# Block 1's square root on ScalarE, block 0 normalised by VectorE and GpSimd side by side, and an order planned with narrower margins

## The chip, the cores and the metric

One core of one Trainium2 chip runs the kernel. The metric is the device time of one execution in microseconds, as the median of several runs. Five engines work in parallel and are tied together by semaphores: TensorE (PE, matmuls; its weight loads are listed apart as PEld), VectorE (DVE), ScalarE (ACT), GpSimd (POOL) and SyncE (SP), which issues most of the DMAs.

## What is computed

```
xn  = layernorm(x)                                   # x: 2 x 4096 x 256, eps 1e-5
h   = tanh(xn @ W1.T + b1);  s = h @ w2 + b2         # scores
e   = exp(s - max(s));  ctx = cumsum(e * xn) / cumsum(e)
att = tanh(concat(ctx, xn) @ Wc.T + bc)
ffn = (silu(xn @ Wg.T) * (xn @ Wu.T)) @ Wd.T         # int32 weights / 127, 768 hidden
out = x + att + ffn
```

All 8192 tokens lie on one core. Float operands are split into a high and a low half-precision part, so that one product in f32 becomes two or three matmuls in f16.

## The kernel before

The tokens are cut into 16 blocks of 512, a block into two pairs of 128-token tiles. The work of a block is cut into steps, each of one engine, named by a kind, the block and a number:

- B (VectorE) takes mean and variance of a pair of tiles, R (VectorE) starts the reciprocal root and T (GpSimd, three Newton rounds) ends it; Ln (ScalarE) or Lp (GpSimd) normalises a pair.
- Lb (TensorE) transposes a pair of blocks 0 and 1, Xh (ScalarE) and Xl (VectorE) take its high and its low half out of PSUM. From block 2 on the halves are made by Xh and Xm (GpSimd) and turned by DMA (Tx, SyncE).
- Ss (ScalarE) seeds a PSUM bank with the bias b1, S (TensorE, 12 matmuls of 256 columns) adds xn @ W1, Th (ScalarE) takes tanh, Sv (VectorE) the product with w2 into a score.
- Gg and Gu (TensorE, 4 matmuls of 512 columns each, six of either kind in a block) are the gate and up products, Sg (ScalarE) silu, H (VectorE) their product, Hh and Hl (ScalarE, VectorE) its halves, D (TensorE) the down product, Da (VectorE) adds it.
- C, Cs, Ct, Ca, N, Sc, Ch, Cl are the same for the context and the second tanh; W1h, W1l, Wgh, Wuh, Wdh turn weights into half precision, K... check them.

The order of each engine's steps is no loop. A planner (`Plan`) runs when the kernel is built: `due_times` gives every step a due time, `needs` says what it must wait for, `STEP` holds its engine, how long it keeps the engine and when its result is seen. `take_one` gives a free engine the earliest due step that is ready. `SLACK` is a margin that a step must leave after its needs once the plan's time is past `STEADY`; `SENT` and `X_SENT` are the times at which weights and x are taken to be there. The steps are then issued in this order on each engine, in order and with semaphore waits; TensorE's order also decides which of the 8 PSUM banks a product uses, and so which earlier step must have freed it.

Ahead of the plan stands a start written out by hand. TensorE runs `WARM` matmuls on constants, spreads the rows b1 and w2 over the partitions by two products with ones (`to_every`), runs `FILL` more matmuls, and then takes the plan's first steps Lb(0,0), Lb(0,1), S(0,0), S(0,1), Gg(0,0). VectorE takes block 0's statistics (`stats_first`), its root with ScalarE's Sqrt in the middle (`root_first`) and normalises its four tiles (`normalise_first`). ScalarE has Sqrt, Copy and Tanh/Silu to run, and loads a table of functions for Sqrt at its start and one for Silu (step Tb).

## Time and profile before

| | us |
|---|---|
| median of 3 runs | 393.72 |
| lowest, highest | 392.94, 393.87 |
| the profiled execution, its own time | 393.06 |
| its span in the profile | 391.1 |
| TensorE busy in the span | 385.9 |

The profile lists one execution. Its own time, 393.06 us, holds 1.96 us that lie around the span of the program's instructions, and stands 0.66 us below the median of the runs. TensorE is busy in 99% of the span; the end of a matmul in the profile is modelled, so the start of the next instruction is the firmer number.

### The profile page before, as it was taken

To read this page: it belongs to the slowest core of one execution; us is meant where nothing else is said; L and a number is where in the kernel's file an instruction comes from. 1 tells how busy PE (TensorE), PEld (TensorE's weight loads), DVE (VectorE), ACT (ScalarE), POOL (GpSimd) and SP (SyncE) were. 2 spreads that over 40 slices of the span, in tenths; PEclk is the share of its full clock that TensorE was granted. 3 is DMA by queue.
4 is the path that set the end of the run, shared out by engine and by line. 5 is a ranking of instruction groups with operands and counts; after the bars stand their busy time and mean duration, and the time that the engine had idled before them with its cause. 6 is when DMAs were issued, how large, how long until landed. Compare 5 with 4: busy or idle time off the path is not lost.

```text
span 391.1 us, 7885 instructions
## 1 busy us (share of the span) xinstructions
PE 385.9 (99%) x2740; PEld 268.7 (69%) x2740; DVE 297.5 (76%) x632; ACT 235.6 (60%) x434; POOL 210.1 (54%) x289
## 2 busy tenths in 40 slices
PE   8999999999999999999999999999999999999996
PEld 4556676757566686866877676767677676676765
DVE  6799998999996997876769966777676765754351
ACT  4766576689985659786556575364553644536250
POOL 1487586874629989794335405866456554502000
PEclk9999999999999999999999999999999999999999
DMA  8944525576834232475210005043231220100001
GB/s 275 348 158 69 137 53 134 106 189 89 201 72 96 54 83 81 116 165 97 76 34 29 27 28 164 28 128 87 58 72 55 90 85 26 54 28 28 28 28 61
DMA packets 54945, 36.56 MB, mean 93 GB/s; under 512 B 31858, under 2 KB 50292, under 8 KB 54900
## 3 DMA queue, kind: packets, MB, share of 16 engines
q1 hardware_dynamic: 54608, 35.73, 35.5%
q8 instruction: 24, 0.39, 0.4%
...
q14 instruction: 21, 0.17, 0.1%
HBM read 20.19 MB, written 8.45 MB: 73 GB/s over the span
## 4 chain that ended last, share of the span: by engine, by line
PE 97%; DVE 2%; issue 0%; DVEq 0%
PE bank L707 44%; PE bank L743 41%; PE bank L763 9%; PE bank L1381 1%; DVE ex L1121 0%; DVE stats L951 0%; PE bank L700 0%; PE bank L1377 0%; DVE veps L980 0%; DVE xt L1091 0%; DVE bank L1116 0%; DVE sg L1413 0%; PE bank L813 0%; DVE mv L955 0%; PE bank L819 0%
## 5 line engine op out<-in xcount | busy, mean ns | idle before, releaser
L743 PE MATMUL bank<-xt,narrow 128*128 128x512 f16 x768 | 177.3, 379 | 0.0
L743 PEld LDWEIGHTS bank<-xt,narrow 128*128 128x128 f16 x768 | 75.2, 98 | 75.4 <-DVE wide L1121 0.2
L707 PE MATMUL bank<-narrow,wide 128*128 128x256 f16 x792 | 96.4, 273 | 0.0
L707 PE MATMUL bank<-narrow,xt 128*128 128x256 f16 x768 | 92.8, 273 | 0.3 <-DVE xt L1091 0.3
L707 PEld LDWEIGHTS bank<-narrow,xt 128*128 128x128 f16 x768 | 75.0, 98 | 19.0 <-DVE xt L1091 0.6
L1258 POOL TENSOR_TENSOR wide<-ex,wide 128x512 f16<-128x512 f32 x32 | 39.4, 1248 | 87.6 <-ACT wide L909 87.6
L888 ACT ACTIVATE sg<-bank 128x512 f32<-128x512 f32 x96 | 57.2, 596 | 46.3 <-PE bank L743 45.6
L1116 DVE SCALAR_TENSOR_TENSOR bank<-bank,sg 128x512 f32<-128x512 f32 x96 | 66.1, 694 | 24.4 <-PE bank L743 21.3
L707 PEld LDWEIGHTS bank<-narrow,wide 128*128 128x128 f16 x792 | 77.5, 98 | 9.4
L895 ACT ACTIVATE wide<-bank 128x512 f16<-128x512 f32 x90 | 53.3, 596 | 47.7 <-DVE bank L1116 39.3
L1121 DVE TENSOR_TENSOR wide<-bank,wide 128x512 f16<-128x512 f32 x90 | 60.5, 678 | 9.9 <-ACT wide L895 8.6
L1139 DVE TENSOR_TENSOR_SCAN ex<-rows,ex 128x512 f32<-128x512 f32 x32 | 56.5, 1767 | 0.7 <-POOL ex L1230 0.7
L1230 POOL TENSOR_TENSOR ex<-ex,rows 128x512 f32<-128x512 f32 x32 | 44.8, 1401 | 9.2 <-DMA rows<-scratch 6.9
L1225 POOL TENSOR_TENSOR ex<-xt 128x512 f32<-128x512 f16 x32 | 44.6, 1395 | 0.2
L1125 DVE TENSOR_TENSOR xres<-bank,xres 128x512 f32<-128x512 f32 (+1 forms) x33 | 22.0, 667 | 26.4 <-PE bank L707 26.3
L841 ACT ACTIVATE bank<-every 128x512 f32<-128x512 f32 (+1 forms) x65 | 38.3, 594 | 0.0
L763 PE MATMUL bank<-narrow,wide 128*128 128x256 f16 x312 | 38.3, 273 | 0.0
L902 ACT ACTIVATE bank<-bank 128x512 f32<-128x512 f32 (+1 forms) x33 | 18.8, 569 | 31.0 <-PE bank L707 31.0
L763 PEld LDWEIGHTS bank<-narrow,wide 128*128 128x128 f16 x312 | 30.5, 98 | 7.4
L1130 DVE TENSOR_TENSOR xres<-bank,xres 128x512 f32<-128x512 f32 x28 | 19.3, 688 | 18.2 <-ACT bank L902 18.1
L1101 DVE CUSTOM_DVE_ANT_0 bank<-bank,every 128x256 f32<-128x256 f32 x64 | 25.4, 446 | 4.1 <-ACT bank L882 4.1
L1244 POOL TENSOR_TENSOR xt<-xnat,xt 128x512 f16<-128x512 f32 x14 | 16.9, 1226 | 11.3 <-ACT xt L869 11.3
...
## 6 DMA issues: line engine op xcount, KB each, us to landing
...
xt<-xt SPq DMA_TRANSPOSE x56, 2.5
...
wide<-in_wc SPq DMA_DIRECT2D x1, 512.0 KB, 11.1
```

The costliest lines, as they stand in the source:

```text
L707: return pe.matmul(dst, lhs, rhs, start=False, stop=stop, skip_group_check=True)
L743: mm = pe.matmul(b[:, :], pg.up(which, k, j), pg.xn(sx, k, tok), start=n == 0, stop=n == len(todo) - 1)
L763: mm = pe.matmul(dst, lhs, rhs, start=n == 0, stop=n == len(todo) - 1)
L841: act.activation(b[:, 0:n * D].rearrange("p (t d) -> p t d", t=n), row.to_broadcast([P, n, D]), ACT.Copy, scale=pg.sum_up).then_inc(done, 1)
L888: act.activation(sg[:, m % SG_RING, :], bank_of(pg, "Gg", i, n)[:, :], ACT.Silu, scale=pg.silu_scale).then_inc(a_sg, 1)
L895: act.activation(pg.h(0, m, slice(0, BLK)), bank_of(pg, "Gu", i, n)[:, :], ACT.Copy).then_inc(a_h, 1)
L1116: dve.scalar_tensor_tensor(out=dst, in0=b[:, :], scalar=pg.up_scale, in1=sg[:, m % SG_RING, :], op0=ALU.mult, op1=ALU.mult).then_inc(v_h, 1)
L1121: dve.tensor_tensor(pg.h(1, m, slice(0, BLK)), bank_of(pg, "Gu", i, n)[:, :], pg.h(0, m, slice(0, BLK)), ALU.subtract).then_inc(v_hlo, 1)
L1139: dve.tensor_tensor_scan(t, rows[:, i % 2, 1, :], t, 0.0 if first else ex[:, (i - 1) % EX_RING, n, BLK - 1:BLK], ALU.mult, ALU.add).then_i ...
L1225: pool.tensor_tensor(dst, xt16[:, 0, k, tok], xt16[:, 1, k, tok], ALU.add).then_inc(g_x, 1)
L1230: pool.tensor_tensor(dst, src, rows[:, i % 2, 0, :], ALU.mult).then_inc(g_ex, 1)
L1258: pool.tensor_tensor(pg.ctx(1, i, k, slice(0, BLK)), ex[:, i % EX_RING, k, :], pg.ctx(0, i, k, slice(0, BLK)), ALU.subtract).then_inc(g_cl ...
```

## The change

Seven things are changed.

- Block 1's reciprocal root is taken as block 0's: ScalarE's Sqrt (a new step Rq) and four small operations on VectorE (`root_first(dve, 1)`), in place of VectorE's integer seed and GpSimd's three Newton rounds T(1,0) to T(1,2).
- Sqrt reads the variance itself and adds eps as its bias, so that VectorE's addition of eps is no longer ahead of it.
- Block 0's tiles are normalised by two engines: VectorE takes tiles 0 and 2, GpSimd tiles 1 and 3.
- The high half of the first pair (Xh(0,0)) is taken tile by tile in two instructions, and S(0,0) starts on the first.
- Rows b1 and w2 go to a bank each (7 and 6), S(0,0) and S(0,1) are seeded straight from the bank that holds b1, and the copies to SBUF (Ea, Eb) come later.
- 9 warm-up matmuls in place of 12, and none between Lb(0,1) and S(0,0).
- The planner gets other numbers: TensorE's margin 0.3 in place of 1.0, valid from 20 in place of 30, Lp at 1.1 in place of 0.75, other times at the start; Tb comes after Rq, and Th of block 0 after Tb.

```
+ROOTS = 2
...
-SLACK, STEADY = {TE: 1.0, SE: 0.3, VE: 0.3}, 30.0
+SLACK, STEADY = {TE: 0.3, SE: 0.3, VE: 0.3}, 20.0
...
-    "T": (PO, 1.35, 1.45), "N": (PO, 3.2, 3.3), "Cl": (PO, 1.2, 1.3), "Lp": (PO, 0.75, 0.85), "Xm": (PO, 1.5, 1.6),
+    "T": (PO, 1.35, 1.45), "N": (PO, 3.2, 3.3), "Cl": (PO, 1.2, 1.3), "Lp": (PO, 1.1, 1.2), "Xm": (PO, 1.5, 1.6),
...
-    "Ea": (SE, 0.5, 0.63), "Tb": (SE, 1.4, 1.5), "W1h": (SE, 0.55, 0.7), "Wch": (SE, 1.06, 1.2), "Kx": (SE, 1.02, 1.2), "Ky": (SE, 1.02, 1.2),
+    "Ea": (SE, 0.3, 0.43), "Eb": (SE, 0.3, 0.43), "Tb": (SE, 1.4, 1.5), "Rq": (SE, 0.2, 0.3), "W1h": (SE, 0.55, 0.7), "Wch": (SE, 1.06, 1.2), "Kx": (SE, 1.02, 1.2), "Ky": (SE, 1.02, 1.2),
...
+ROW_BANKS = (BANKS - 1, BANKS - 2)
+BEGIN = {TE: 7.0, SE: 5.95, VE: 7.3, PO: 7.4, SY: 12.0}
+SENT = {"W1h": 6.4, "Ea": 6.1, "Eb": 6.6, "Wgh": 8.8, "Wuh": 12.3,
         "Wdh": 22.0, "K1": 36.0, "Kc": 38.0, "Wch": 50.0}
...
-X_SENT = (0.0, 11.1, 20.0)
...
+X_SENT = (0.0, 10.3, 20.0)
...
-    if kind in ("W1h", "Wgh", "Ea"):
+    if kind in ("W1h", "Wgh"):
         return []
+    if kind == "Ea":
+        return [(("Xh", 0, 1), 0)]
+    if kind == "Eb":
+        return [(("Ea", 0, 0), 0)]
     if kind == "Tb":
-        return [(("Xh", 0, 1), 0)]
+        return [(("Xh", 0, 1), 0), *((("Rq", g, 0), 0) for g in range(1, ROOTS))]
+    if kind == "Rq":
+        return [(("B", i, 1), 0)]
...
-        return [(("B", blocks[-1], 1), 0), *([(("R", i - 1, 0), 0)] if i > 1 else [])]
+        return [(("Rq", i, 0) if i < ROOTS else ("B", blocks[-1], 1), 0), *([(("R", i - 1, 0), 0)] if i > 1 else [])]
...
-        return [(("T", g, NEWTON - 1), 0), *frees, *([(("C", 1, 1), 0)] if i == SPARE_TO - 1 and not wide else [])]
+        return [(("T", g, NEWTON - 1) if g >= ROOTS else ("R", g, 0), 0), *frees, *([(("C", 1, 1), 0)] if i == SPARE_TO - 1 and not wide else [])]
...
+        return [(("S", i, x), 0), *([] if i or wide else [(("Tb", 0, 0), 0)])]
...
-            pe.wait_ge(*(pg.norm_ready(i, pr) if i or pg.wide else (v_xn, pr + 1)))
+            if i or pg.wide:
+                pe.wait_ge(*pg.norm_ready(i, pr))
+            else:
+                pe.wait_ge(v_xn, pr + 1)
+                pe.wait_ge(g_x0, pr + 1)
...
-                if by_halves:
+                first = by_halves and (i, pr) == (0, 0)
+                if first:
+                    pe.wait_ge(a_x0, 1)
+                elif by_halves:
...
+                        if first and t and not (sx or sw):
+                            pe.wait_ge(a_x, pg.nth("Xh", i, pr))
...
+        def spread_row(act, pg, row, b, done, n=2):
+            row = row.rearrange("p (t d) -> p t d", t=1)
             act.activation(b[:, 0:n * D].rearrange("p (t d) -> p t d", t=n), row.to_broadcast([P, n, D]), ACT.Copy,
                            scale=pg.sum_up).then_inc(done, 1)
+
+        def square_root(act, g):
+            act.wait_ge(v_mv, 2 * g + 2)
+            act.activation(rstd[:, columns(g)], mv[:, columns(g), 1], ACT.Sqrt, bias=eps[:, 0:1]).then_inc(a_root, 1)
...
+            elif kind == "Xh" and (i, n) == (0, 0) and not pg.wide:
+                act.wait_ge(p_x, pg.nth("Lb", i, n))
+                turned = half(bank_of(pg, "Lb", i, n)[:, :])
+                act.activation(xt16[:, 0, :, 0:P], turned[:, :, 0:P], ACT.Copy, scale=X_UP).then_inc(a_x0, 1)
+                act.activation(xt16[:, 0, :, P:2 * P], turned[:, :, P:2 * P], ACT.Copy, scale=X_UP).then_inc(a_x, 1)
...
-                act.wait_ge(a_b, 1)
                 act.wait_ge(p_warm, 1)
-                bias_seed(act, pg, 0, open_bank(act, pg, "S", i, n), a_ss)
+                if i or pg.wide:
+                    act.wait_ge(a_b, 1)
+                    bias_seed(act, pg, 0, open_bank(act, pg, "S", i, n), a_ss)
+                else:
+                    act.wait_ge(p_b, 1)
+                    spread_row(act, pg, bank[ROW_BANKS[0]][:, 0:D], open_bank(act, pg, "S", i, n), a_ss)
...
-                act.activation(every[:, 0:2 * D], bank[BANKS - 1][:, :], ACT.Copy).then_inc(a_b, 1)
+                act.activation(b1_every, bank[ROW_BANKS[0]][:, 0:D], ACT.Copy).then_inc(a_b, 1)
+            elif kind == "Eb":
+                act.wait_ge(p_b, 2)
+                act.activation(w2b, bank[ROW_BANKS[1]][:, 0:D], ACT.Copy).then_inc(a_b, 1)
+            elif kind == "Rq":
+                square_root(act, i)
...
-        def root_first(dve):
-
-            t, n = columns(0), [0]
+        def root_first(dve, g):
+
+            t, n = columns(g), [ROOT_STEPS_DVE * g]
 
             def step(ins):
                 n[0] += 1
                 ins.then_inc(v_rs0, 1)
                 dve.wait_ge(v_rs0, n[0])
 
-            dve.wait_ge(v_mv, 2)
-            step(dve.tensor_scalar(veps[:, t], mv[:, t, 1], EPS, None, ALU.add))
-            dve.tensor_scalar(minus_half[:, t], veps[:, t], -0.5, None, ALU.mult)
-            dve.wait_ge(a_root, 1)
+            dve.wait_ge(v_mv, 2 * g + 2)
+            dve.tensor_scalar(minus_half[:, t], mv[:, t, 1], EPS, -0.5, ALU.add, ALU.mult)
+            dve.wait_ge(a_root, g + 1)
...
-        def normalise_first(dve, pr):
-            dve.wait_ge(v_rs0, ROOT_STEPS_DVE)
-            for t in range(2):
-                c = 2 * pr + t
-                ins = dve.tensor_scalar(xnat[:, pr, t, :], xres[:, c, :], mv[:, c, 0:1], rstd[:, c:c + 1],
-                                        ALU.subtract, ALU.mult)
-            ins.then_inc(v_xn, 1)
+            return (g_rs, ROOT_STEPS * (g - ROOTS + 1)) if g >= ROOTS else (v_rs0, ROOT_STEPS_DVE * (g + 1))
+
+        def normalise_first(eng, c, done):
+
+            eng.wait_ge(v_rs0, ROOT_STEPS_DVE)
+            eng.tensor_scalar(xnat[:, c // 2, c % 2, :], xres[:, c, :], mv[:, c, 0:1], rstd[:, c:c + 1],
+                              ALU.subtract, ALU.mult).then_inc(done, 1)
...
-                root_seed(dve, i)
+                root_seed(dve, i) if i >= ROOTS else root_first(dve, i)
...
-            to_every(bank[BANKS - 1], 0, b_row)
-            to_every(bank[BANKS - 1], D, w2_row).then_inc(p_b, 1)
-
-            spare_bank = next(FITS.place["Gg", 0, j] for j in range(KH) if FITS.before["Gg", 0, j] is None and FITS.place["Gg", 0, j] < BANKS - 1)
+            to_every(bank[ROW_BANKS[1]], w2_row)
+
+            spare_bank = FITS.place["Lb", 0, 0]
             for n in range(FILL):
                 warm_up(spare_bank)
             pe.wait_ge(s_ident, 16)
             for kind, i, n in FITS.early(TE):
                 tensor_step(pe, fits, kind, i, n)
-                if (kind, i, n) == ("Lb", 0, 1):
-                    for n in range(FILL):
-                        warm_up(spare_bank)
...
+            for c in (1, 3):
+                normalise_first(pool, c, g_x0)
...
-            root_first(dve)
-            for pr in range(2):
-                normalise_first(dve, pr)
+            root_first(dve, 0)
+            for c in (0, 2):
+                normalise_first(dve, c, v_xn)
...
```

ScalarE, from block 0's root (ahead of the fence stand table load and DMA issues) to the first Th. Before: root, W1h, the rows' copy, Ss(0,0), Xh(0,0) and Xh(0,1), Ss(0,1), Tb, Th.

```order
L1368 ACTIVATE rstd<-veps 128x4
L917 ACTIVATE narrow<-wide 128x512
L912 ACTIVATE every<-bank 128x512
L841 ACTIVATE bank<-every 128x512
L873 ACTIVATE xt<-bank 128x2x256 x2
L841 ACTIVATE bank<-every 128x512
L914 ACT_TABLE_LOAD
L914 ACTIVATE spare<-one 128x1
L882 ACTIVATE bank<-bank 128x512 x2
```

After, the same stretch to Tb, with L870 for the seeds and L875 for the roots:

```order
L875 ACTIVATE rstd<-mv,eps 128x4
L870 ACTIVATE bank<-bank 128x512
L964 ACTIVATE narrow<-wide 128x512
L906 ACTIVATE xt<-bank 128x2x128
L907 ACTIVATE xt<-bank 128x2x128
L911 ACTIVATE xt<-bank 128x2x256
L870 ACTIVATE bank<-bank 128x512
L954 ACTIVATE every<-bank 128x256
L957 ACTIVATE every<-bank 128x256
L875 ACTIVATE rstd<-mv,eps 128x4
L961 ACT_TABLE_LOAD
L961 ACTIVATE spare<-one 128x1
```

The seed of S(0,0) has moved ahead of W1h, the copy of the rows behind Ss(0,1) and into two, and block 1's root stands ahead of the second table load, which itself stands ahead of every Th and Sg as before.

TensorE, from the rows b1 and w2 to the first scores S(0,0). Before:

```order
L1377 MATMUL bank7<-sg,ones 128x256 x2
L1381 MATMUL bank4<-sg 128x512 x2
L700 MATMUL bank0<-ident,xnat 128x128 x4
L700 MATMUL bank2<-ident,xnat 128x128 x4
L1381 MATMUL bank4<-sg 128x512 x2
L707 MATMUL bank1<-narrow,xt 128x256 x12
```

After:

```order
L1425 MATMUL bank7<-sg,ones 128x256
L1425 MATMUL bank6<-sg,ones 128x256
L1428 MATMUL bank1<-sg 128x512 x2
L721 MATMUL bank1<-ident,xnat 128x128 x4
L721 MATMUL bank2<-ident,xnat 128x128 x4
L728 MATMUL bank0<-narrow,xt 128x256 x12
```

The rows have banks of their own, and the two filling matmuls ahead of S(0,0) are gone.

TensorE, from Gu(0,2) on: L743 and L769 are Gg and Gu, L700 and L721 the transposes Lb(1,0) and Lb(1,1), L707 and L728 the scores. Before:

```order
L743 MATMUL bank1<-xt,narrow 128x512 x4
L743 MATMUL bank3<-xt,narrow 128x512 x4
L743 MATMUL bank0<-xt,narrow 128x512 x4
L743 MATMUL bank4<-xt,narrow 128x512 x4
L743 MATMUL bank5<-xt,narrow 128x512 x4
L700 MATMUL bank6<-ident,xnat 128x128 x4
L700 MATMUL bank0<-ident,xnat 128x128 x4
L743 MATMUL bank1<-xt,narrow 128x512 x4
L707 MATMUL bank7<-narrow,xt 128x256 x12
L707 MATMUL bank2<-narrow,xt 128x256 x12
```

After, from the same Gu(0,2):

```order
L769 MATMUL bank0<-xt,narrow 128x512 x4
L721 MATMUL bank2<-ident,xnat 128x128 x4
L721 MATMUL bank3<-ident,xnat 128x128 x4
L769 MATMUL bank6<-xt,narrow 128x512 x4
L769 MATMUL bank7<-xt,narrow 128x512 x4
L728 MATMUL bank1<-narrow,xt 128x256 x12
L769 MATMUL bank2<-xt,narrow 128x512 x4
L769 MATMUL bank5<-xt,narrow 128x512 x4
L769 MATMUL bank7<-xt,narrow 128x512 x4
L728 MATMUL bank4<-narrow,xt 128x256 x12
```

Block 1's transposes have moved ahead of four gate and up products (Gu(0,3), Gg(0,4), Gu(0,4), Gg(0,5)), and three such products now stand between S(1,0) and S(1,1), which were side by side.

Further on TensorE's order differs at a few more places, at each by one or two products (D(0,0), D(1,0), D(2,0), D(5,0) and C(1,0) come earlier, M1(1,0) ahead of D(8,0)); its last 117 of 302 steps stand as before, as do VectorE's last 134 and ScalarE's last 139. GpSimd loses T(1,0) to T(1,2), SyncE's first 20 steps are the same.

## Rows read from the trace of the kernel before

**Rows 1.** The page, part 1: busy time and instructions by engine.
```profile
PE 385.9 (99%) x2740; PEld 268.7 (69%) x2740; DVE 297.5 (76%) x632; ACT 235.6 (60%) x434; POOL 210.1 (54%) x289
```

**Rows 2.** All waits of TensorE in the span: us in total, times, longest.
```profile
PE bank L1381 <- DVE sg L1413: 1.5, 1, 1.5
PE bank L707 <- DVE xt L1091: 0.3, 1, 0.3
```

**Rows 3.** Timeline of TensorE, 1.4 to 12.3: start, us, what.
```profile
1.52 4.66 PE L1381 MATMUL bank<-sg 128*128 128x512 f16 x12 [1.52 <-DVE sg L1413]
6.11 1.13 PE L1377 MATMUL bank<-sg,ones 1*128 1x256 f32 x4
...
7.62 1.21 PE L700 MATMUL bank<-ident,xnat 128*128 128x128 f32 x8
...
9.12 2.78 PE L707 MATMUL bank<-narrow,xt 128*128 128x256 f16 x24
11.74 0.81 PE L743 MATMUL bank<-xt,narrow 128*128 128x512 f16 x3
```

**Rows 4.** Timeline of VectorE, the same stretch.
```profile
5.42 0.17 DVE L1014 TENSOR_SCALAR veps<-mv 128x4 f32<-128x4 f32 x1
...
6.74 1.38 DVE L1031 TENSOR_SCALAR xnat<-xres,mv,rstd 128x256 f32<-128x256 f32 x4
...
9.05 1.29 DVE L1091 SCALAR_TENSOR_TENSOR xt<-bank,xt 128x512 f16<-128x512 f32 x2 [0.33 <-ACT xt L873]
10.26 0.74 DVE L951 BATCH_NORM_STATS2 stats<-xres 128x6 f32<-128x256 f32 x2
11.04 0.25 DVE L955 BATCH_NORM_AGGREGATE mv<-stats 128x2 f32<-128x6 f32 x2
```

**Rows 5.** Timeline of ScalarE, the same stretch.
```profile
5.63 0.20 ACT L1368 ACTIVATE rstd<-veps 128x4 f32<-128x4 f32 x1 [1.62 <-DVE veps L1014]
6.43 0.63 ACT L917 ACTIVATE narrow<-wide 128x512 f16<-128x512 f32 x1 [0.60 <-DMA wide<-in_w]
...
7.90 0.60 ACT L841 ACTIVATE bank<-every 128x512 f32<-128x512 f32 x1
8.44 1.07 ACT L873 ACTIVATE xt<-bank 128x512 f16<-128x512 f32 x2
9.40 0.60 ACT L841 ACTIVATE bank<-every 128x512 f32<-128x512 f32 x1
10.02 1.28 ACT L914 ACT_TABLE_LOAD   x1
...
11.42 1.10 ACT L882 ACTIVATE bank<-bank 128x512 f32<-128x512 f32 x2
```

**Rows 6.** Timeline, 374 to 392: an activation over 256 columns.
```profile
377.47 0.40 ACT L841 ACTIVATE bank<-every 128x256 f32<-128x256 f32 x1
```

**Rows 7.** Lines L1031 and L1239: ns min/median/max, starts, forms.
```profile
L1031 DVE TENSOR_SCALAR xnat<-xres,mv,rstd x4: 405/406/411, 6.7 to 7.7; 128x256 f32<-128x256 f32 x4
...
L1239 POOL TENSOR_SCALAR xnat<-xres,rstd,shift x20: 556/561/565, 19.5 to 82.0; 128x256 f32<-128x256 f32 x20
```

**Rows 8.** Timeline of GpSimd, 1.4 to 12.3.
```profile
8.66 1.48 POOL L1249 TENSOR_SCALAR narrow<-wide 128x1536 f16<-128x1536 int32 x1 [8.22 <-DMA wide<-in_wg]
12.11 1.48 POOL L1252 TENSOR_SCALAR narrow<-wide 128x1536 f16<-128x1536 int32 x1 [1.97 <-DMA wide<-in_wu]
```

**Rows 9.** Timeline of all engines, 21 to 25.
```profile
21.23 1.24 PE L700 MATMUL bank<-ident,xnat 128*128 128x128 f32 x8
...
21.78 1.47 POOL L1255 TENSOR_SCALAR narrow<-wide 128x1536 f16<-128x1536 int32 x1
...
22.30 1.03 PE L743 MATMUL bank<-xt,narrow 128*128 128x512 f16 x4
22.43 0.85 DVE L980 TENSOR_SCALAR veps<-mv 128x4 f32<-128x4 f32 x1
...
23.17 1.04 PE L707 MATMUL bank<-narrow,xt 128*128 128x256 f16 x8
...
24.54 0.72 PE L707 MATMUL bank<-narrow,xt 128*128 128x256 f16 x5 [0.33 <-DVE xt L1091]
```

**Rows 10.** Busy time of VectorE in a stretch: length, busy (instructions), clock.
```profile
40.00:60.00 20.00, 19.05 (x60) 1.00 0.38 89
```

More of the change, by code:

```diff
@@ L187, in due_times @@
             due["R", g, 0] = root
-            for n in range(NEWTON):
+            if g < ROOTS:
+                due["Rq", g, 0] = root
+            for n in range(NEWTON * (g >= ROOTS)):
                 due["T", g, n] = root + 0.1 + 1.4 * n
@@ L298, in needs @@
     if kind == "Ss" and i == 0 and not wide:
-        return [(("Ea", 0, 0), 0), *([(("Xh", 0, 0), 0)] if x else [])]
+        return [(("Xh", 0, 0), 0)] if x else []
+    if kind == "Ss" and i == 1 and not wide:
+        return [(("Ea", 0, 0), 0)]
     if kind in ("Gg", "Gu"):
@@ L362, in __init__ @@
         self.place, self.before, self.held = {}, {}, dict.fromkeys(range(BANKS))
-        self.whole = {n: not wide and n < BANKS - 1 for n in range(BANKS)}
-        self.open_now, self.freed = set(), {n: 9.0 if n == BANKS - 1 else 0.0 for n in range(BANKS)}
+        self.whole = {n: not wide and n not in ROW_BANKS for n in range(BANKS)}
+        self.open_now, self.freed = set(), {n: 11.0 if n in ROW_BANKS else 0.0 for n in range(BANKS)}
         self.behind, self.freed_behind = set(), set()
@@ L1375, in _, with to_every @@
             pe.wait_ge(v_set, 2)
-            def to_every(b, at, row):
-                return pe.matmul(b[:, at:at + row.shape[1]], ones[0:1, :], row, start=at == 0, stop=True,
-                                 skip_group_check=True)
+            def to_every(b, row):
+                return pe.matmul(b[:, 0:D], ones[0:1, :], row, start=True, stop=True).then_inc(p_b, 1)
             def warm_up(n):
```

77 lines of the change are left out of this document (41 added, 36 removed).

## The prediction

> **What bounds the kernel now.** I read the page's busy times first: TensorE has work in 385.9 of 391.1 us, every other engine in 76% or less [rows 1]. The list of TensorE's waits then says how much of the rest is waiting: after the 1.5 us at the start there is a single wait of 0.3 us, on VectorE's Xl [rows 2]. So the span is three pieces: the time until the first scores S(0,0), which start at 9.12 [rows 3]; a string of matmuls that hardly ever breaks; and a tail behind the last one. The change leaves the products as they are, and TensorE's last 117 steps stand in the same order, so tail and string keep their length. What can change is when S(0,0) starts, what is lost inside the string before, and what new gaps the new order opens.
>
> **The start, step by step.** Before, the chain to S(0,0) runs through VectorE and ScalarE. The variances are there shortly before 5.42; eps is added until 5.59, ScalarE takes the root from 5.63, and the first tile is normalised from 6.74 [rows 4, 5]. Four tiles take 1.38 us [rows 4], 0.33 apart. The first transposes start at 7.62 [rows 3], 0.14 behind the end of tile 1 (6.74 + 0.33 + 0.41 = 7.48). Their high half is taken at 8.44, and not sooner, because ScalarE is seeding until 8.50 [rows 5]. S(0,0) follows 0.1 behind its end.
>
> After:
> - The root starts when the variances are there, 0.2 earlier. All that hangs on it moves with it: normalising starts at 6.54.
> - GpSimd takes tile 1. It needs 0.56 for such a tile [rows 7], so it ends at about 7.14; VectorE's tile 0 ends at 6.95. The transposes start at 7.28. Two tiles on two engines save only 0.14 here, as GpSimd is slower; tile 3 ends at 7.70, and the second transposes start at 7.83.
> - The seed of S(0,0) needs the row b1 spread in a bank. That product is ready at 6.2: nine warm-up matmuls end 3 x 0.22 to 3 x 0.43 sooner than twelve, and it is half of the 1.13 us of the rows [rows 3]. Seed until 6.8, W1h (0.63 [rows 5]) until 7.5: ScalarE is now idle when the first four transposes (half of 1.21 [rows 3]) end at about 7.95.
> - A half of Xh(0,0) takes 0.40, by the activation over 256 columns [rows 6]. S(0,0) starts at 7.95 + 0.40 + 0.10 = 8.45, that is 0.67 earlier.
> - Some is given back at once. The second half lands at 8.70, seen at 8.80, where TensorE could go on at 8.67: 0.12. Xl(0,0) (0.69, two of them in 1.29 [rows 4]) can start only behind it, at 8.73, is seen at 9.51, and is wanted at 9.44: 0.07. Scores of block 0 end 2.81 after their start, at 11.26. Gg(0,0) started at 11.74 before [rows 3]. **Lead: 0.48 us.**
> - Wgh and Wuh wait for weights, not for this: they end at 10.14 and 13.59 [rows 8], and are wanted at 11.26 and four products later, 14.71. The two filling matmuls that go away ran in time that nobody wanted.
>
> **Block 1.** Before, two gaps stand there. Between 21.23 and 22.30 stand eight transposes, 8 x 0.11 = 0.87 of work: 0.20 lost, since Lp(1,1) on GpSimd has just ended when Lb(1,1) is wanted. In S(1,0), eight matmuls from 23.17 end by 24.04 and the ninth starts at 24.54: 0.50 lost on Xl(1,0) [rows 9]. That Xl stood behind an addition over four columns that took 0.85 us in place of 0.17, and ended when GpSimd's weight conversion did (21.78 + 1.47 = 23.25) [rows 4, 9]. Together 0.70.
>
> After, block 1's root needs no Newton rounds. The statistics of block 1 follow Xl(0,1): two pairs, each about 1.0 (10.26 to 11.29 [rows 4]), until 12.05. ScalarE idles from 10.5, takes the root until 12.3, loads the table (1.28 [rows 5]) and starts Th(0,0) 1.40 behind the start of that load: 13.65, which is 2.2 later than before. This is the wait that the change adds; queued behind it are Th(0,0), Th(0,1), Sg(0,0) to Sg(0,2), Ss(1,0), each some 0.5 behind the other. Who waits: Gu(0,2) uses the bank of S(0,0) and is wanted at 11.26 + 6 x 0.865 = 16.45; Sv(0,0) frees it at 15.1. Lb(1,0), wanted at 17.3, needs Sg(0,1), at 15.8. Gg(0,4), at 19.1, needs Sg(0,3), at 17.8. So 1.3 us or more is spare at each. Xh(1,0) is ready at 18.7 and Xl(1,0) at 20.1, wanted at 20.0 and 20.8. VectorE's queue up to Sv(1,1), counted out at 0.6 to 1.0 us a step, ends near 27.6, wanted by Gu(1,1) at 27.8: the tightest. I take both old gaps as closed, **0.70 us**, since the transposes now find their normalised tiles a full microsecond early and the weight conversion falls in a stretch without such an addition.
>
> **The margins.** TensorE now leaves 0.3 after its needs in the plan where it left 1.0. VectorE is busy 19.05 of 20 us from 40 on [rows 10], so a delay there is not made good soon. The list of waits shows no wait after 24.54 with the old margin. I allow 0.1 us for new gaps, between nothing and 0.7 (the margin given up, once).
>
> **The sum** against the profiled execution: -0.48 - 0.70 + 0.10 = -1.08, that is 393.06 to 392.0. The median of the runs lies 0.66 above this execution. One thing can explain part of that. The column of the granted clock shows full speed here, but the twelve warm-up matmuls took 4.66 us, 0.39 on average, where three later ones of the same shape take 0.22 each [rows 3]: most of them ran at the lower level (1.2 GHz), and the level rose near the end. If in another execution it rises later, twelve matmuls, rows and fills at 0.43 hold the first transposes back to some 9.3, by 1.7 us; nine hold them to 8.1, by 0.8. The change then saves 0.9 more. I take 0.25 of it for the median: 393.72 - 1.08 - 0.25 = **392.4**. The range starts at 391.6 (0.55 more from that, 0.25 from gaps that I have not counted) and ends at 393.7 (nothing gained).
>
> **Rivals.**
> - *New gaps eat the gain* (0.17). VectorE's and GpSimd's order is new from 12 to 110 us; where VectorE's addition meets a GpSimd operation it loses 0.7 us, as at 22.43 [rows 9], and with 0.2 us spare at Gu(1,1) half a microsecond reaches TensorE. One or two such meetings leave 393.0 to 393.7.
> - *The two engines don't work side by side* (0.04). If the tile on GpSimd cannot start before VectorE's first has ended (6.95), it ends at 7.51, and the transposes start at 7.65; if it waits for both, at 7.99. The lead shrinks from 0.48 to 0.11 or less, and the median to 392.8 or 393.1. Against it: VectorE's tile of 256 columns takes 0.406 [rows 7] and its operation on 4 columns 0.17 [rows 4], so 0.94 ns a column, one column at a time, while the operation that was held up at 22.43 is the kind without per-partition operands.
> - *Slower* (0.05): the root on ScalarE comes too late. Block 1's x lands at or before 10.26 now [rows 4]. Every engine behind Th has 1.3 us spare; from there each further microsecond is lost once. To end over 0.3% slower the root must come 1.3 + 1.1 + 1.2 = 3.6 us later than I have it, at 15.9. A landing at 13.7 would do that.
> - *Nothing changes* (0.02): TensorE held by something else at 9.1, such as a late row or late weights; 393.7.
>
> The Trainium skill, "SBUF — State Buffer", Who interferes with whom, says that VectorE's tensor_scalar may use the port pair that it shares with GpSimd, and that the second of two such operations then fully blocks. By that rule the second rival would hold, 392.8 to 393.1; the 0.85 us at 22.43 agrees with the rule, the 0.406 us of a tile speaks against it for this operation. The same section says that a VectorE operation with two inputs in SBUF blocks against a GpSimd operation that reads SBUF: root_first(1) would then wait for Wuh until 13.6 and Lp(1,1) end at 16.5, ahead of 17.3, so the sum would stay.
>
> My forecast, faster by 0.2 to 0.55%, has 0.72, and its own range is 391.6 to 393.0. About 0.3%, 1.2 us, is what a measurement of this kernel can tell from no change; two thirds of the forecast's chance lie beyond it. With the rivals: faster 0.48, within 0.45, slower 0.07.
>
> **What the profile would show.** Right: GpSimd's two tiles start within 0.1 of VectorE's first and take 0.56; first transposes near 7.3; S(0,0) near 8.45; Gg(0,0) near 11.3; Th(0,0) near 13.7 without TensorE waiting in 16 to 20; no gap near S(1,0); the last matmul 1.0 to 1.2 earlier. Wrong: a tile on GpSimd that ends after 7.4; a wait of TensorE on Sv(1,1) or on a bank near 28; any wait of over 0.3 later; VectorE additions of over 0.8 us ahead of steps that TensorE wants.

## The result

After: 395.69 us, median of 7 runs (394.88 to 396.16), against 393.72 before (392.94 to 394.10). The ratio is 1.0056, with an interval of 1.0046 to 1.0067: slower by 0.56%. The forecast was 392.4 us, with a range of 391.6 to 393.7.

The page of the changed kernel's profiled execution (396.15 us, span 394.3), parts 1, 2 and 5. TensorE is busy 386.6 us where it was 385.9 [rows 1], in a span that is 3.2 us longer:

```profile
span 394.3 us, 7862 instructions
## 1 busy us (share of the span) xinstructions
PE 386.6 (98%) x2735; PEld 269.0 (68%) x2735; DVE 296.6 (75%) x631; ACT 235.0 (60%) x437; POOL 212.6 (54%) x277
```

TensorE's waits over the whole span (us in total, times, longest), to be set beside [rows 2]. All but the 1.6 at the start are new, and they name GpSimd's tiles and small operations of VectorE:

```profile
PE bank L721 <- POOL xnat L1076: 1.6, 2, 1.0
PE bank L1428 <- DVE sg L1460: 1.6, 1, 1.6
PE bank L721 <- POOL xnat L1285: 0.3, 1, 0.3
PE bank L832 <- DVE mxb L1093: 0.3, 1, 0.3
PE bank L769 <- DVE sm L1097: 0.2, 1, 0.2
```

TensorE's timeline from 1 to 14.5 us, which answers to [rows 3] (start, us, engine and line, what):

```profile
1.55 4.02 PE L1428 MATMUL bank<-sg 128*128 128x512 f16 x9 [1.55 <-DVE sg L1460]
5.50 1.13 PE L1425 MATMUL bank<-sg,ones 1*128 1x256 f32 x4
6.56 0.61 PE L1428 MATMUL bank<-sg 128*128 128x512 f16 x2
8.12 0.63 PE L721 MATMUL bank<-ident,xnat 128*128 128x128 f32 x4 [0.95 <-POOL xnat L1076]
9.38 1.08 PE L721 MATMUL bank<-ident,xnat 128*128 128x128 f32 x4 [0.63 <-POOL xnat L1076]
10.26 3.80 PE L728 MATMUL bank<-narrow,xt 128*128 128x256 f16 x24
13.89 0.81 PE L769 MATMUL bank<-xt,narrow 128*128 128x512 f16 x3
```

The first transposes start at 8.12, not at 7.28, and wait 0.95 us for GpSimd; the second four wait 0.63 for it again. Then the 24 matmuls of the scores take 3.63 us from start to the next product, where they took 2.62 before. The groups of GpSimd's instructions up to 25 us say why the transposes wait:

```profile
L1285 POOL TENSOR_SCALAR xnat<-xres,mv,rstd 128x256 f32<-128x256 f32 x4 | 4.8, 1219 | 0.6 <-DVE rstd L1066 0.6
L1076 POOL TENSOR_SCALAR xnat<-xres,mv,rstd 128x256 f32<-128x256 f32 x2 | 2.6, 1302 | 6.2 <-DVE rstd L1066 6.2
```

A tile on GpSimd takes 1.22 to 1.34 us, not the 0.56 of [rows 7]. And a table of stretches (length, busy us of PE, PEld, DVE, ACT and POOL with their instructions, granted clock, DMA) says why the scores are slow. Behind the first pause, and inside the second, the granted clock falls to half, 1.2 GHz. In the trace it is low from 8.92 to 12.33 us, and the matmuls' durations double and halve with it:

```profile
8.00:9.00 1.00, 0.63 (x4) 0.42 (x4) 0.14 (x1) 0.21 (x1) 1.00 (x1) 0.96 1.06 400
9.00:10.00 1.00, 0.62 (x3) 0.65 (x4) 0.52 (x1) 0.45 (x2) 0.23 (x1) 0.50 1.02 410
10.00:11.00 1.00, 1.00 (x7) 0.73 (x6) 0.17 (x1) 0.50 (x2) 0.92 (x1) 0.50 1.03 372
11.00:12.00 1.00, 1.00 (x7) 0.67 (x6) 0.87 (x2) 1.00 (x4) 0.56 (x1) 0.50 1.08 364
```

This fall was no exception. With that low stretch the mean granted clock of the execution is 0.996, and five of the seven runs of the changed kernel have that mean, the profiled one among them. Of the kernel before 80 further runs stand beside the experiments, none with less than 0.998. (A level that rises late at the start leaves no mark in this mean, as run 7 will show.)

**Where the time went**, in the two profiled executions. Gg(0,0) starts 2.15 us later (13.89 against 11.74): 1.14 from the later start of the scores, 1.01 from their slower pace. At block 1 the two gaps of 0.17 and 0.49 are gone, and one of 0.44 is new, at Lb(1,1), which waits for GpSimd's tile: 0.22 won. Two late gaps are new, 0.36 at 102.8 and 0.44 at 220.2 (of such gaps the start of the matmul ahead of them is given). Sum 2.73 (2.15 - 0.22 + 0.36 + 0.44); the last matmul starts 2.76 later. The end of the program stands 0.45 further behind that matmul, a distance that lies between 3.7 and 4.1 us in the fourteen traces. That makes the 3.2 us of the two spans; the medians lie 1.97 apart, since the profiled run before was at the low end of its runs and the one after at the high end.

The second late gap in the timeline of all engines. VectorE's copy of 128 columns starts while GpSimd is at its two-input operations, takes 0.90 us where the same copy near 98 takes 0.23, and TensorE's transposition waits for it:

```profile
218.35 2.27 POOL L1307 TENSOR_TENSOR wide<-ex,wide 128x512 f16<-128x512 f32 x2 [5.64 <-ACT wide L951]
...
219.80 0.90 DVE L1093 COPY mxb<-sm 128x128 f32<-128x128 f32 x1
...
220.85 0.30 PE L832 MATMUL bank<-ident,mxb 128*128 128x128 f32 x1 [0.27 <-DVE mxb L1093]
```

GpSimd's pair ends at 220.62 and the copy at 220.70. The hold-up itself is not new. In the kernel before the copy takes as long, but the transposition comes 2.3 us behind its end:

```profile
217.51 0.91 DVE L1049 COPY mxb<-sm 128x128 f32<-128x128 f32 x1
...
220.74 0.27 PE L806 MATMUL bank<-ident,mxb 128*128 128x128 f32 x1
```

So what is new at 220 is TensorE's order, which leaves no room behind the copy. At 102.8 VectorE's reduction (L1097) comes too late for TensorE. Two operations over 8 columns are held some steps ahead of it, for 0.72 us at 99.66 and 1.08 at 100.41; in the kernel before one of them was (0.88 at 100.51), and no gap followed. That they make the gap is argued, not shown (in run 9, which has no such gap, the reduction comes first).

### The profile page after: what moved, and what is told of

The parts are those of the page before. It is cut to its first block, busy times and chain, and to the rows that moved or that the text cites. A ratio compares the mean times of both kernels' runs of the same rounds, so it can differ in the third digit from the quotient of the medians.

```text
span 394.3 us, 7862 instructions
## 1 busy us (share of the span) xinstructions
PE 386.6 (98%) x2735; PEld 269.0 (68%) x2735; DVE 296.6 (75%) x631; ACT 235.0 (60%) x437; POOL 212.6 (54%) x277
## 3 DMA queue, kind: packets, MB, share of 16 engines
HBM read 20.19 MB, written 8.45 MB: 73 GB/s over the span
## 4 chain that ended last, share of the span: by engine, by line
PE 78%; DVE 15%; issue 3%; POOL 1%; DMA 1%; ACT 0%; DVEq 0%; POOLq 0%
PE bank L728 37%; PE bank L769 33%; PE bank L789 8%; DVE stats L998 3%; DVE bank L1160 2%; DVE wide L1165 2%; DVE bank L1145 2%; POOL xnat L1285 1%; DVE mv L1002 1%; DMA xres<-in_x 1%; DVE xt L1207 1%; POOL xnat L1076 1%; PE bank L721 0%; DVE xres L1169 0%; DVE score L1145 0%
## 5 line engine op out<-in xcount | busy, mean ns | idle before, releaser
L769 PE MATMUL bank<-xt,narrow 128*128 128x512 f16 x768 | 177.8, 379 | 0.2 <-DVE sm L1097 0.2
L769 PEld LDWEIGHTS bank<-xt,narrow 128*128 128x128 f16 x768 | 75.1, 98 | 75.5 <-DVE sm L1097 0.7
L728 PE MATMUL bank<-narrow,wide 128*128 128x256 f16 x792 | 96.4, 273 | 0.0
L728 PE MATMUL bank<-narrow,xt 128*128 128x256 f16 x768 | 94.0, 274 | 0.0
L728 PEld LDWEIGHTS bank<-narrow,xt 128*128 128x128 f16 x768 | 75.7, 99 | 19.1
L728 PEld LDWEIGHTS bank<-narrow,wide 128*128 128x128 f16 x792 | 77.5, 98 | 9.4
L1275 POOL TENSOR_TENSOR ex<-ex,rows 128x512 f32<-128x512 f32 x32 | 42.4, 1325 | 14.4 <-DMA rows<-scratch 12.2
L1270 POOL TENSOR_TENSOR ex<-xt 128x512 f32<-128x512 f16 x32 | 46.4, 1449 | 0.2
L870 ACT ACTIVATE bank<-every 128x512 f32<-128x512 f32 (+1 forms) x63 | 37.1, 593 | 0.0
L924 ACT ACTIVATE bank<-bank 128x512 f32<-128x512 f32 x32 | 18.5, 582 | 7.3 <-PE bank L728 7.2
```

What stands on the lines that cost most here:

```text
L728: return pe.matmul(dst, lhs, rhs, start=False, stop=stop, skip_group_check=True)
L769: mm = pe.matmul(b[:, :], pg.up(which, k, j), pg.xn(sx, k, tok), start=n == 0, stop=n == len(todo) - 1)
L870: act.activation(b[:, 0:n * D].rearrange("p (t d) -> p t d", t=n), row.to_broadcast([P, n, D]), ACT.Copy, scale=pg.sum_up).then_inc(done, 1)
L1270: pool.tensor_tensor(dst, xt16[:, 0, k, tok], xt16[:, 1, k, tok], ALU.add).then_inc(g_x, 1)
L1275: pool.tensor_tensor(dst, src, rows[:, i % 2, 0, :], ALU.mult).then_inc(g_ex, 1)
```

## The experiments

Theory A: the form of GpSimd's tiles (subtract, then multiply) makes them slow, and that delays both blocks. Theory B: the low clock is a cost of its own, by the pauses or by the shorter warm-up. Theory C: TensorE's narrower margin opens the late gaps. Rival to A: two engines side by side hold each other up, whatever the form. The kernel before was run again beside them: its median was 393.32 us beside runs 1 to 4, 393.43 beside runs 5 to 8 and 393.44 beside runs 9 to 12. The ratios are to these; their intervals reach 0.4 to 0.7 us to either side, so a gain of less than that over the changed kernel is not told from none by the medians. The probe (8) is a single run. Runs 8 and 10 start from the kernel before, the others from the changed kernel.

**1. VectorE normalises all four tiles of block 0.**

```diff
-            for c in (1, 3):
-                normalise_first(pool, c, g_x0)
...
-            for c in (0, 2):
+            for c in range(4):
                 normalise_first(dve, c, v_xn)
```

> VectorE normalises all four tiles of block 0, GpSimd none; the rest as after the change (395.69 us). Theory A, GpSimd's subtract-and-multiply form itself costs 1.2 to 1.3 us a tile: the first transposes start near 7.5 in place of 8.12, S(0,0) near 8.7 in place of 10.26, Gg(0,0) near 11.5 in place of 13.89, and TensorE keeps its full clock; but block 1's tiles, still in that form (4 x 1.22 us), are now wanted 2.4 us earlier and open a gap of 1.0 to 2.5 us at Lb(1,0) or Lb(1,1), so the time is 394.0 to 395.3. Rival B, the tile is slow because VectorE works beside it: the same start, but GpSimd's tiles of block 1 are short where VectorE is idle. Rival C, the start costs nothing and only later gaps do: 395.5 or more.

Measured: 394.93 us (394.33 to 395.92), ratio 1.0038 [1.0027, 1.0049]. Transposes at 7.27, scores at 8.42, Gg(0,0) at 11.13: 0.6 ahead of the kernel before, with a warm-up of nine, and TensorE never slow after 6.02. So the delay at the start goes once GpSimd is out of it. The gain is lost again at block 1, where GpSimd's four tiles, still in the slow form, can start only behind the root, at 14.72, and end at 19.57. TensorE's longest wait:

```profile
PE bank L720 <- POOL xnat L1284: 1.8, 1, 1.8
```

**2. GpSimd's tiles of blocks 0 and 1 multiply, then add** (the shift of -mean times root costs VectorE one more operation over four columns).

```diff
+            step(dve.scalar_tensor_tensor(out=shift[:, t], in0=mv[:, t, 0], scalar=-1.0, in1=rstd[:, t],
+                                          op0=ALU.mult, op1=ALU.mult))
...
-                    if i < ROOTS:
-                        ins = pool.tensor_scalar(..., mv[:, c, 0:1], rstd[:, c:c + 1], ALU.subtract, ALU.mult)
-                    else:
-                        ins = pool.tensor_scalar(..., rstd[:, c:c + 1], shift[:, c:c + 1], ALU.mult, ALU.add)
+                    ins = pool.tensor_scalar(..., rstd[:, c:c + 1], shift[:, c:c + 1], ALU.mult, ALU.add)
```

> GpSimd normalises blocks 0 and 1 in the multiply-and-add form that it uses for all later blocks, with the shift from one more small VectorE operation (0.2 us) in the root. Theory A (the form): each tile on GpSimd takes 0.56 us also beside VectorE, first transposes near 7.6, S(0,0) near 8.7, Gg(0,0) near 11.6, no gap or one under 0.6 at Lb(1,1); 392.8 to 393.6 us. Rival B (VectorE beside it): tiles of block 0 stay at 1.2 to 1.3 us and the time within 0.4 of 395.69.

Measured: 394.87 us (393.18 to 395.88, 12 runs), ratio 1.0031 [1.0017, 1.0045], above the 392.8 to 393.6 expected. GpSimd's pair takes 1.25 us instead of 2.60, and block 1 has no gap. But in the profiled run the level was low until 10.9, and TensorE paid that before the transposes (start, us, what):

```profile
5.50 2.07 PE L1427 MATMUL bank<-sg,ones 1*128 1x256 f32 x4
7.51 1.03 PE L1430 MATMUL bank<-sg 128*128 128x512 f16 x2
8.34 1.91 PE L721 MATMUL bank<-ident,xnat 128*128 128x128 f32 x8
```

Two runs lie at 393.2, the others between 394.75 and 395.88; four of these have a mean granted clock of 0.996, so the level fell back in them. Theory A holds for the tiles. What is left in the trace is the clock (B) and the two late gaps (C).

**3. TensorE's margins back at 1.0 and 30.**

```diff
-SLACK, STEADY = {TE: 0.3, SE: 0.3, VE: 0.3}, 20.0
+SLACK, STEADY = {TE: 1.0, SE: 0.3, VE: 0.3}, 30.0
```

> Only the planner's margin of TensorE is back at 1.0 us from 30 on. If the narrower margin opened the two late gaps (0.36 us near 103 and 0.44 us near 220), they go and the time falls by 0.6 to 0.9, to 394.8 to 395.1; the start stays as it was (S(0,0) near 10.3). If they come from the start or from chance, the time stays within 0.3 of 395.69.

Measured: 395.69 us (395.03 to 396.11), ratio 1.0051 [1.0035, 1.0067]. Both late gaps are gone, and two others are there instead: 0.69 us at 34.7, ahead of D(0,0), and 0.26 near 109. The sum is much the same (0.95 where it was 0.80), and so is the time. A margin of 1.0 only moves the loss in this order. (Not every margin does: run 9, at 0.6, has no such gap.) The copy at 220 is held here too, for 0.89 us, but TensorE's transposition comes 2.3 us behind it, as in the kernel before. So theory C holds for that gap.

**4. Filling matmuls: six ahead of the transposes, three between them, two behind** (they write to bank 4, by a line not shown).

```diff
-            for n in range(FILL):
+            for n in range(6):
                 warm_up(spare_bank)
...
                 tensor_step(pe, fits, kind, i, n)
+                if kind == "Lb" and i == 0:
+                    for _ in range(2 if n else 3):
+                        warm_up(spare_bank)
```

> Filling matmuls keep TensorE at work while it waits for the tiles: 6 in place of 2 ahead of Lb(0,0), 3 behind it, 2 behind Lb(0,1). GpSimd's slow tiles stay. Theory C, the lower clock adds about 1 us: the clock stays at full from 5 to 13, S(0,0) starts near 10.1, the scores of block 0 take 2.8 us and not 3.6, Gg(0,0) starts near 12.9; 394.6 to 395.0 us. If the clock is not what stretches them, 395.5 to 395.9.

Measured: 395.34 us (394.61 to 396.27), ratio 1.0045 [1.0027, 1.0062]. The pauses are filled but for 0.43 us, the level stays full from 5.85 on, the scores take 2.62 us, and Gg(0,0) starts at 13.05 instead of 13.89. So the low clock behind the pauses was a cost of its own. But Lb(1,1) now waits 0.58 instead of 0.44 for the slow tiles of block 1. The last matmul starts 0.69 sooner than in the changed kernel; the medians, 395.34 and 395.69, don't tell that from no change.

**5. The form, and the margins back** (edits 2 and 3 together).

> The changed kernel with GpSimd's tiles of blocks 0 and 1 in the multiply-add form and TensorE's margins back at 1.0 and 30. Theory 1 (form, clock and margins are separate costs): the two late gaps of 0.36 and 0.45 us near 101.5 and 218.9 go, block 1 stays without a gap, the clock still depends on how the warm-up falls; from 394.87 with the form alone, less 0.8 us: 394.1 us. Theory 2 (wide margins only move the gaps elsewhere, as the 0.69 us near 34.7 in the run with margins alone): 394.7 to 395.0 us, with a gap of about 0.7 us at block 1's D and one of 0.3 near 109.

Measured: 394.85 us (393.33 to 396.00), ratio 1.0036 [1.0022, 1.0050], the time of edit 2 alone: theory 2 of the expectation. The gap of 0.70 near 34 in the timeline of all engines shows the same meeting as at 220: an operation over four columns takes 0.99 us beside GpSimd's pair (30.93 to 33.20), and the subtraction that D(0,0) needs (Hl, L1171) comes that much later:

```profile
30.93 2.27 POOL L1295 TENSOR_TENSOR xt<-xnat,xt 128x512 f16<-128x512 f32 x2 [0.25 <-ACT xt L902]
...
32.23 0.99 DVE L1027 TENSOR_SCALAR veps<-mv 128x4 f32<-128x4 f32 x1
33.26 0.17 DVE L1028 TENSOR_SCALAR minus_half<-veps 128x4 f32<-128x4 f32 x1
...
33.73 0.69 DVE L1171 TENSOR_TENSOR ex<-bank,ex 128x512 f16<-128x512 f32 x1
...
34.48 0.50 PE L789 MATMUL bank<-narrow,ex 128*128 128x256 f16 x3 [0.54 <-DVE ex L1171]
```

In five of the ten runs, the profiled one among them, the level fell back (mean clock 0.996). And here the rival has a part: GpSimd's second tile of block 0, in the short form, took 1.10 us instead of 0.56, beside VectorE's W1l (0.67 us from 7.52), which has two inputs in SBUF; in run 4 the slow form took 1.67 instead of 1.26 there.

**6. The form, and fillings** (edit 2; as edit 4, with four, one and two).

> The changed kernel with GpSimd's tiles in the multiply-add form, 4 filling matmuls ahead of the first transposes (2 before), 1 between the pairs and 2 behind them. If the clock of the warm-up is a cost of its own: granted clock full from about 6 us on, transposes from about 7.6, scores from 9.2 in 2.6 us, Gg(0,0) from 12.0 (13.09 with the form alone), so 1.0 us less than the slow group of that run: 393.8 to 394.1 us, with the late gaps of 0.36 and 0.45 still there. If the fillings only delay the transposes by as much as they save: 394.6 to 394.9 us.

Measured: 394.83 us (393.39 to 397.12, 12 runs), ratio 1.0035 [1.0019, 1.0051]. Six runs are at 393.4 to 394.4, six at 395.2 to 397.1. The median is in the expectation's second range. Fillings work both ways: those that fall in a wait cost nothing, but every other one holds TensorE back, by 0.43 us in the profiled run, where the level is low until 13.43, and by 0.22 in run 4, where it is full and the two behind the transposes hold up the scores (10.00 to 10.43).

**7. VectorE for all tiles of block 0, the form for block 1, margins back, fillings** (edits 1, 2, 3, and those of 6).

> VectorE normalises all four tiles of block 0, GpSimd's tiles of block 1 are in the multiply-add form, margins 1.0 and 30, fillings 4, 1 and 2. If the three causes are all there is: Gg(0,0) at about 11.4 us (11.74 before), the clock full from about 6 us, no gap at Lb(1,1), no gaps of 0.36 and 0.44 near 102 and 219; 0.3 us ahead of the kernel before at block 0 and 0.66 at block 1: 392.4 to 392.9 us, faster than before by 0.4 to 0.9. If the order with new costs has gaps of its own that come back wherever the work is put (0.7 near 34.7, 0.3 near 109): 393.4 to 394.0 us, no better than before.

Measured: 393.68 us (393.14 to 397.20, 12 runs), ratio 1.0012 [0.9995, 1.0029]. Ten runs lie at 393.1 to 393.8; two, one of them the profiled run, at 397.0 and 397.2. The time falls in the second range of the expectation, and its reason is in the trace: the gaps of margin 1.0 are back, 0.70 us ahead of D(0,0) at 36.85 and 0.25 near 110. The profiled run's timeline shows the low level at its dearest:

```profile
1.55 4.02 PE L1425 MATMUL bank<-sg 128*128 128x512 f16 x9 [1.55 <-DVE sg L1459]
5.51 2.07 PE L1422 MATMUL bank<-sg,ones 1*128 1x256 f32 x4
7.51 1.89 PE L1425 MATMUL bank<-sg 128*128 128x512 f16 x4
9.19 1.06 PE L720 MATMUL bank<-ident,xnat 128*128 128x128 f32 x4
...
12.18 2.07 PE L727 MATMUL bank<-narrow,xt 128*128 128x256 f16 x12
```

TensorE had no pause of over 0.2 us from 1.55 on, and yet a matmul of 512 columns took 0.427 us up to 12.2, and one of 256 columns 0.21 until 13.4, where it halves. A wait is not needed for a late rise. The column of the granted clock reads 1.00 in that stretch, so at the start of a trace the durations have to be read instead.

**8. The probe: eight GpSimd operations at the start of the kernel before**, each over 128x256. pa is a column with a stride; pb isn't used, pc and pd are columns side by side; their setup isn't shown.

```diff
+            for x, y, o, q in ((pa, pd, sub, mul), (pc, pd, sub, mul), (pc, pd, add, mul), (pa, pd, mul, add), (pc, pd, mul, add),
+                               (pc, pd, mul, sub), (0.5, 2.0, sub, mul), (2.0, 0.5, mul, add)):
+                n_probe += 1
+                pool.tensor_scalar(po, pin, x, y, o, q).then_inc(g_probe, 1)
+                pool.wait_ge(g_probe, n_probe)
```

> The kernel before with eight extra GpSimd operations at its start, each 128x256 f32 to f32, their output used by nobody: subtract-multiply with two per-partition scalars (first scalar taken from a strided, then from a contiguous tensor), add-multiply, multiply-add (strided, contiguous), multiply-subtract, and subtract-multiply and multiply-add with two constants. If the order of the two operations makes GpSimd slow: 1.2 us for every one that begins with subtract or add, 0.56 for those that begin with multiply. If the strided scalar does: 1.2 us for the two with a strided scalar and 0.56 for the others. If it is subtraction alone: 1.2 for the subtract forms and 0.56 for add-multiply.

Measured, in GpSimd's timeline, in the order of the list (subtract-multiply twice, add-multiply, multiply-add twice, multiply-subtract):

```profile
1.24 1.23 POOL L1418 TENSOR_SCALAR ex<-ex,pcol,pflat 128x256 f32<-128x256 f32 x1
...
2.56 1.22 POOL L1418 TENSOR_SCALAR ex<-ex,pflat 128x256 f32<-128x256 f32 x1
...
3.89 0.56 POOL L1418 TENSOR_SCALAR ex<-ex,pflat 128x256 f32<-128x256 f32 x1
...
4.54 0.56 POOL L1418 TENSOR_SCALAR ex<-ex,pcol,pflat 128x256 f32<-128x256 f32 x1
...
5.21 0.56 POOL L1418 TENSOR_SCALAR ex<-ex,pflat 128x256 f32<-128x256 f32 x1
...
5.87 1.23 POOL L1418 TENSOR_SCALAR ex<-ex,pflat 128x256 f32<-128x256 f32 x1
```

It is the subtraction, first or second; neither the order nor the stride of the scalar matters. VectorE was idle from 1.62 to 3.38, and the first subtract-multiply, from 1.24, took 1.23 all the same, so this is no hold-up between the two. (From 3.38 on VectorE was at its statistics.) With constants in place of the columns it was 1.14 (subtract-multiply) and 0.92 (multiply-add); there VectorE was at work on its tiles, so these two are not clean.

**9. VectorE for all tiles of block 0, the form for block 1, twelve warm-up matmuls, no fillings, margin 0.6.** The margin was chosen by the planned order, to have no such small operation held right ahead of TensorE.

```diff
-SLACK, STEADY = {TE: 0.3, SE: 0.3, VE: 0.3}, 20.0
+SLACK, STEADY = {TE: 0.6, SE: 0.3, VE: 0.3}, 20.0
...
-        WARM, FILL = 9, 2
+        WARM, FILL = 12, 0
```

> VectorE normalises all four tiles of block 0, GpSimd's tiles of block 1 are in the multiply-add form, 12 warm-up matmuls as before and no filling ones, TensorE's margin 0.6. If a long warm-up makes the level rise before the transposes in every run and the three causes are all there is: transposes at 7.3 to 7.6 us, Gg(0,0) at 11.3 to 11.5 (11.74 before), level full from 4.4 to 6 us in every run, no gap at Lb(1,1), none over 0.2 us near 34, 102 and 220: 392.5 to 392.9 us, and no run over 394.5. If small VectorE operations are again held by a GpSimd one somewhere: a gap of 0.36 to 0.7 us, and 393.2 to 393.5. If the warm-up's length does not matter: some runs at 395 to 397 as in the run with all three.

Measured: **392.42 us** (392.09 to 394.04, 12 runs), ratio 0.9980 [0.9969, 0.9991] to the kernel before. Gg(0,0) starts at 11.64, GpSimd's four tiles of block 1 take 2.17 us, and the list of TensorE's waits has one row left, the start:

```profile
PE bank L1425 <- DVE sg L1455: 1.6, 1, 1.6
```

The copy near 217 is held here too (0.89 us), but its transposition comes 2.3 us behind it. Near 100 an addition is held for 0.50 us, behind the reduction that TensorE wants and not ahead of it. The start is a little later than expected, since the level rose at 6.33. One of the twelve runs, at 394.04, has a mean clock of 0.996.

**10. The kernel before with nine warm-up matmuls.**

```diff
-        WARM, FILL = 12, 2
+        WARM, FILL = 9, 2
```

> The kernel before with 9 warm-up matmuls instead of 12 and nothing else. If the shorter warm-up is what keeps the clock low in the changed kernel: part of the runs at 393.1 to 393.5 us, part 0.9 us and more above the kernel before, up to 395 to 397, in groups. If only TensorE's idle time behind the warm-up does (waits for GpSimd's tiles, of which this kernel has none): no group above the kernel before, median 393.1 to 393.5 us.

Measured: 394.12 us (392.72 to 395.93, 12 runs), ratio 1.0014 [0.9998, 1.0030]. Five runs at 392.7 to 393.4, six at 394.0 to 394.8, one at 395.9; the kernel before has 30 runs between 392.87 and 394.11. The median rises 0.7, though the interval still touches 1. The mean granted clock tells the groups apart: it is 0.996 in all of the five runs from 394.03 to 394.56, and 1.00 in the other seven. So in those five the level fell back. That the two at 394.80 and 395.93 had a late rise is inferred from the traces of 2, 6 and 7. The profiled run, 393.37 us, has the level full from 6.14, but also a pause that the kernel before doesn't have, because three matmuls fewer stand ahead of it (and because its variances came 0.38 later):

```profile
8.01 1.21 PE L700 MATMUL bank<-ident,xnat 128*128 128x128 f32 x8 [0.56 <-DVE xnat L1031]
```

So the expectation's premise, that this kernel has no idle time behind the warm-up, is false, and the run doesn't part the shorter warm-up from the pauses: the one brings the other.

**11. The changed kernel with twelve warm-up matmuls** (WARM = 12, nothing else).

> The changed kernel with 12 warm-up matmuls instead of 9 and nothing else. If the shorter warm-up cost it the clock: the level full through the scores of block 0 (2.62 us for 24 instead of 3.63), Gg(0,0) at 13.0 instead of 13.89, so 394.7 to 395.0 us. If the waits for GpSimd's slow tiles cost it (idle 0.95 and 0.6 us): the level falls again near 9, and 395.5 to 395.9 us.

Measured: 395.20 us (394.44 to 396.01), ratio 1.0044 [1.0029, 1.0059]. The time lies between the two expected ranges, and isn't told from the changed kernel's by the medians. The trace is as expected for the shorter warm-up: the level is full from 5.38 on and stays so in spite of pauses of 0.24 and 0.58 us, and Gg(0,0) starts at 12.37, 1.5 earlier. (The longer warm-up also shortens the first pause, from 0.95. One run of seven, at 396.01, still has a mean clock of 0.996.) But 0.68 of it is given back at once: the slow tiles of block 1 come little sooner, and the gap at Lb(1,1) grows from 0.44 to 1.12 (timeline of TensorE):

```profile
18.41 0.60 PE L721 MATMUL bank<-ident,xnat 128*128 128x128 f32 x4
19.97 0.63 PE L721 MATMUL bank<-ident,xnat 128*128 128x128 f32 x4 [0.96 <-POOL xnat L1285]
```

**12. As 9, but GpSimd takes tiles 1 and 3 of block 0, multiply-add.**

> As the run before the last but one (12 warm-up matmuls, no fillings, margin 0.6, multiply-add on GpSimd), but GpSimd takes tiles 1 and 3 of block 0, as in the change, in the multiply-add form. If two engines side by side are worth what two short tiles are: first pair ready about 0.1 us sooner and the second 0.3 sooner than with VectorE alone, but one more VectorE operation ahead, so the same within 0.2 us: 392.4 to 393.0 us. If GpSimd's hold on VectorE costs more than that, 0.3 us or more behind the run with VectorE alone.

Measured: 392.76 us (392.15 to 394.00, 12 runs), ratio 0.9986 [0.9975, 0.9997]. Gg(0,0) at 11.55 instead of 11.64. A tile on GpSimd takes 0.585 and 0.681 us here and one on VectorE beside it 0.414 and 0.502 (0.41 alone). The two engines do work side by side, and it is worth nothing that these runs can tell. The slower tiles use part of it up, and VectorE's W1l beside GpSimd's second tile takes 0.86 us instead of 0.69. The operation for the shift doesn't count: it stands ahead of the tiles in run 9 too. In run 9 the transposes, at 7.64, came right behind the last matmul of the rows, so sooner tiles had nothing to win there.

## Why the prediction was wrong

- **The step that failed: "GpSimd takes tile 1. It needs 0.56 for such a tile [rows 7]".** That row is of a multiply-add; the tile added is a subtract-multiply, and takes 1.26 to 1.34. The text called the two "such a tile", and gave no bound for an operation that the trace of before didn't show on GpSimd. The planner had the same price (Lp, a pair of tiles, at 1.1; it took 2.4). The end of tile 3 moves from 7.70 to 9.23, the second transposes from 7.83 to 9.38. Runs 1, 2 and 8 show it.
- **The same number at block 1.** "I take both old gaps as closed": the two old gaps did go (0.66), but GpSimd's four tiles take 4.83 us where four multiply-add ones take 2.17 (run 9), and 0.44 came back; where the start was on time it was 1.95 (run 1). The wait on the root itself was harmless, as argued: Th(0,0) started at 15.44, not 13.65, and TensorE never waited for Th or for what hangs on it. VectorE's first operation with two SBUF inputs there took 1.01 us beside Wuh (13.78 to 15.26), which the Trainium skill, "SBUF — State Buffer", Who interferes with whom, foretold.
- **"The change then saves 0.9 more" took the clock to be the same with nine warm-up matmuls as with twelve.** I saw that the level rises at different times, and held a shorter warm-up to be cheaper whenever it rises late. Run 10 shows a loss in its place: with nine matmuls part of the runs lose 0.6 to 2.5 us, five by a level that falls back and two, as inferred, by a late rise. In the changed kernel the level fell back behind pauses that the forecast didn't have, and that was 1.0 of the 2.15 us at the start (scores of 3.63 against 2.62). The case of the forecast itself, a late rise with twelve, stands in no trace: in the five with twelve the level is full by 6.33 at the latest. The Trainium skill, "TensorE: Matmul & The Clock Gate", Part 1, says that how many first matmuls are slow differs between runs of one kernel. The traces agree: the full level began at 5.39 in the kernel before, and in versions with nine warm-ups, whose first fifteen matmuls are the same, at 4.44, 5.50, 6.02 and 10.9, and at 13.4 in two. No kernel has two traces here.
- **"I allow 0.1 us for new gaps"** was 0.80 here. The mechanism is in part the one of the first rival (VectorE's small operations meet a GpSimd one), which had only 0.17. But at 220 such an operation was held before as well; what the narrower margin took away is the room behind it. So the reason given, the margin, was right there, though a margin of 1.0 has 0.96 us of gaps elsewhere in this order (runs 3 and 5), and one of 0.6 none (runs 9 and 12).
- The rival that the engines don't work side by side is refuted for these tiles: in the changed kernel and in run 12 GpSimd's tile starts within 0.01 us of VectorE's, and VectorE's take 0.41 to 0.50 us. Beside W1l there is a hold-up (runs 5 and 12). The rival on the slower side named the root as the cause; it ended slower by a cause that none named.
- **The root** was taken to start "0.2 earlier", and normalising at 6.54. It did start 0.21 earlier, but took 0.30 us instead of 0.20, and normalising started at 6.63. Two terms are also a little larger than what they are added from: 6.54 + 0.56 is 7.10, not 7.14, and 7.28 with half of 1.21 is 7.89, not 7.95.
- Right, and in part by luck: run 1 has transposes at 7.27 (7.28 forecast), S(0,0) at 8.42 (8.45), Gg(0,0) at 11.13 (11.26). With VectorE alone the forecast's own steps give 7.42 for the transposes, and in that execution the variances came 0.24 sooner than in the kernel before. What it bears out is the length of the steps from the transposes on: 1.15 us to S(0,0) (1.17 forecast) and 2.71 of scores (2.81).
- Run 9's 392.42 us stands at the forecast's 392.4 by luck, not by its terms: in its trace the start gains 0.10 us and not 0.48 (Gg(0,0) at 11.64, since twelve warm-up matmuls keep TensorE busy), block 1 the 0.66, and the last matmul starts 0.80 sooner than before.

**Open:** why the level fell again behind a pause of 0.95 us in the changed kernel, 0.92 in run 3 and 0.93 in run 5, and not behind 0.24 and 0.58 in run 11, 0.56 in run 10 or 0.71 in run 12. How much of the gain of run 9 is its margin and how much its warm-up was not separated.
